# A two-layer conditioned feed-forward kernel: block products for pairs of tiles in place of one tile's dense product

## The reference

```python
x = x + _L0_ffn_ref(_L0_cond_ref(x, ...), ...)
x = x + _L1_ffn_ref(_L1_cond_ref(x, ...), ...)
# _L0_cond_ref: grouped convolution of 9 taps in 4 groups of channels + a row that depends on the sample
# _L0_ffn_ref:  h @ W.T + b, and a low-rank term of which a router picks rank 8, 16, 32 or 64 for each row
# _L1_cond_ref: a 64 x 64 mixing matrix per sample, a softmax mixture of 8, + a bias
# _L1_ffn_ref:  h @ W_base.T + b_base, and 8 experts of rank 16, weighted by a sparsemax router
```

## Time and profile before

| what | value |
|---|---|
| median of three runs (lowest, highest) | 545.91 us (543.35, 546.39) |
| span of the profiled execution | 542.1 us; a time of its own is not given, the median is 3.8 us above its span |
| TensorE matmul busy | 535.2 us, 99% |
| VectorE, ScalarE, GpSimd busy | 243.1, 80.8, 7.6 us |
| bytes by DMA | 56.46 MB, mean 104 GB/s |

### The profile page before, as it was taken

The page is one execution under the profiler, slowest core; times in us unless marked ns, Lnnn a source line. Parts: engine busy times, 40 slices in busy tenths (PEclk is TensorE's granted clock), DMA queues, the critical chain, the costliest instruction groups (busy, mean ns, idle before and its releaser), DMA issues.

```text
span 542.1 us, 9035 instructions
## 1 busy us (share of the span) xinstructions
PE 535.2 (99%) x3401; PEld 532.1 (98%) x3401; DVE 243.1 (45%) x635; ACT 80.8 (15%) x173; POOL 7.6 (1%) x25
## 2 busy tenths in 40 slices
PE   8989999999999999999999999999999999999997
PEld 8989999999999999999999999999999999999997
DVE  1964334344334343343467645454335454434543
ACT  3731101111011111011152100111100111100010
POOL 3010000000000000000000000000000000000000
PEclk9999999999999999999999999999999999999999
DMA  8997633223233222232210222012222102222201
GB/s 271 328 414 236 238 115 118 85 77 109 77 116 116 78 78 96 97 116 81 74 41 39 79 79 77 15 63 77 77 77 77 44 33 77 77 77 77 77 39 40
DMA packets 16057, 56.46 MB, mean 104 GB/s; under 512 B 1915, under 2 KB 3067, under 8 KB 15916
## 3 DMA queue, kind: packets, MB, share of 16 engines
q1 hardware_dynamic: 15980, 56.23, 30.2%
q0 software_dynamic: 64, 0.05, 0.1%
HBM read 39.47 MB, written 16.79 MB: 104 GB/s over the span
## 4 chain that ended last, share of the span: by engine, by line
PE 93%; DMA 4%; ACT 1%; issue 1%; DVE 1%; SPq 0%; POOL 0%; DVEq 0%; POOLq 0%
PE mixp L713 9%; PE acc_a L703 8%; PE acc_a L705 8%; PE acc_a L704 8%; PE acc_b L704 8%; PE acc_b L705 8%; PE acc_b L703 8%; PE acc_c L703 8%; PE acc_c L704 8%; PE acc_c L705 8%; PE mixp L736 5%; DMA w_raw<-in_wcat 2%; DMA ctx_scratch<-ctx_sb 1%; DMA rw<-in_rows 1%; PE utp L756 1%
## 5 line engine op out<-in xcount | busy, mean ns | idle before, releaser
L703 PE MATMUL acc_a<-w_hi,act_hi 128*128 128x388 f32 (+1 forms) x248 | 85.6, 345 | 0.0
L705 PE MATMUL acc_a<-w_hi,act_lo 128*128 128x388 f32 (+1 forms) x248 | 82.8, 334 | 0.0
L704 PE MATMUL acc_a<-w_lo,act_hi 128*128 128x388 f32 (+1 forms) x248 | 82.8, 334 | 0.0
L705 PE MATMUL acc_b<-w_hi,act_lo 128*128 128x388 f32 (+1 forms) x248 | 82.7, 333 | 0.0
L704 PE MATMUL acc_c<-w_lo,act_hi 128*128 128x384 f32 (+1 forms) x248 | 82.7, 333 | 0.0
L704 PE MATMUL acc_b<-w_lo,act_hi 128*128 128x388 f32 (+1 forms) x248 | 82.7, 333 | 0.0
L703 PE MATMUL acc_b<-w_hi,act_hi 128*128 128x388 f32 (+1 forms) x248 | 82.7, 333 | 0.0
L705 PE MATMUL acc_c<-w_hi,act_lo 128*128 128x384 f32 (+1 forms) x248 | 82.6, 333 | 0.0
L703 PE MATMUL acc_c<-w_hi,act_hi 128*128 128x384 f32 (+1 forms) x248 | 82.5, 333 | 0.0
L713 PE MATMUL mixp<-filt,blk 128*128 128x128 f32 x512 | 63.3, 283 | 0.8 <-DMA filt<-in_toep 0.8
L713 PEld LDWEIGHTS mixp<-filt,blk 128*128 128x128 f32 x512 | 62.2, 199 | 0.9 <-DMA blk<-in_xblk 0.9
(11 more groups left out here) (148 smaller groups left out, 521.0 us busy)
## 6 DMA issues: line engine op xcount, KB each, us to landing
blk<-in_xblk SPq DMA_DIRECT2D x16, 516.0 KB, 3.3
xs<-in_x SPq DMA_DIRECT2D x16, 512.0 KB, 3.3
x_scratch<-xs SPq DMA_DIRECT2D x16, 512.0 KB, 2.7
blk<-x_scratch SPq DMA_DIRECT2D x16, 512.0 KB, 4.0
out_dram<-xs SPq DMA_DIRECT2D x15, 512.0 KB, 4.7
w_raw<-in_wcat SPq DMA_DIRECT2D x8, 580.0 KB, 17.0
w_raw<-in_wcat SPq DMA_DIRECT2D x8, 546.0 KB, 7.6
lb_raw<-in_bcat SPq DMA_DIRECT2D x2, 512.0 KB, 13.6
```

Of the source, the lines that this page charges most:

```text
L703: pe.matmul(dst, l_hi, r_hi, start=start, stop=False, skip_group_check=skip)
L704: pe.matmul(dst, l_hi, r_lo, start=False, stop=False, skip_group_check=skip)
L705: return pe.matmul(dst, l_lo, r_hi, start=False, stop=stop, skip_group_check=skip)
```

## The change

Tiles go in pairs: pair g has tiles 2g and 2g+1; pairs 0 to 7 are layer 0, 8 to 15 layer 1. The two tiles' 256 rows, the 1024 inputs in two halves, and 864 (layer 1: 928) output columns in two halves of 432 (464) make a 2 by 2 block product. Pairs 1 to 15 make it with seven products of 12 matmuls each (4 blocks of 128 rows, 3 terms) in place of eight (Strassen's algorithm in Winograd's form). The other 228 (232) columns, with the router's, stay a plain product (`plain`). Pair 0 is still made in the ordinary way (`dense0`).

- Sums of activations, four of 128 x 512 for each pair, are made on GpSimd (`sums`) in place in `mixed`; ScalarE and VectorE split each into hi and lo as they do the activations.
- Sums of layer 0's weights, 16 of 128 x 432, are made on GpSimd behind the split of `lb`; ScalarE and VectorE split them (`split_t`).
- Sums and splits of layer 1's weights are made during pairs 1 to 6, by GpSimd and ScalarE in turn (`prep`), and stored in HBM by ScalarE's queue, 28 blocks of 128 x 464, then 6 of the plain columns and 3 of `lb`. SyncE loads them at the boundary: two halves (hi, lo) of seven slots of 128 x 4 x 464 and of the plain part, 950 KB each, and `lb`.
- Each product's result is added to `xs` by VectorE at once, or left in its bank for the next product; layer 1's mixing matrices (`place_kernels`) go through HBM too.
- In layer 1 GpSimd adds `b_base` to the loaded `x` (`add_base`).
- The loads of `rw` and `bk` are issued by ScalarE, and the context's matmuls are five in place of three.

Constants, and the order of TensorE before and after:

```diff
+HALF = (432, 464)
+PLAIN = (W0COLS - 2 * HALF[0], W1COLS - 2 * HALF[1])
+B11, T3, B21, B22, T1, T2, T4 = range(7)
+PREP_JOBS = ((), ((0, B11), (2, B21)), ((3, B22), (0, T1)), ((1, T3), (3, T2)), ((2, T4),))
+PREP_BASE = 5 * HK
+PREP_STEPS = PREP_BASE + 6
+PREP_FIRST, PREP_LAST = 1, 6
+PREP_A_PAIR = 5
...
-    for k in range(NCH):
-        act_ready(T, k)
-        if k == 0:
-            if mixed_out is None:
-                pe.wait_ge(res_done[PART_C], T - 1)
-        ins = dense(s, cols, PART_C, k)
-    ins.then_inc(hid_done, 1)
...
-    for k in range(NCH):
-        dense(s, cols, PART_A, k)
-        if k == (NCH - 2 if following is not None else NCH - 4):
-            turn_u(T)
-    if following is not None:
-        following(T + 1, 1 - s, pair + s)
-    lora(T, s, PART_C)
-    lora(T, s, PART_A)
-    pe.wait_ge(res_done[PART_B], T)
-    for k in range(NCH):
-        dense(s, cols, PART_B, k)
-    lora(T, s, PART_B)
...
+turn_u(0)
+for k in range(3, 6):
+    dense0(1, k, second)
+pe.wait_ge(lblo_done, 1)
+pe.wait_ge(bias_split, 1)
+h = HALF[0]
+lora(0, b_x, 0, h, c11_done)
+lora(0, b_y, h, 2 * h, c12_done)
+lora(0, b_p[0], 2 * h, D, q_done[0])
+for k in range(6, NCH):
+    dense0(1, k, second)
+conv_half(2, 0, b_m)
+pe.wait_ge(fin11, 1)
+conv_half(2, 1, b_x)
+turn_u(1)
+pe.wait_ge(fin12, 1)
+aggregate(0, b_y)
+lora(1, b_z, 0, h, c21_done)
+lora(1, b_w, h, 2 * h, c22_done)
+lora(1, b_p[1], 2 * h, D, q_done[1])
+pe.wait_ge(sum_done, 5)
+conv_half(3, 0, b_m)
+pe.wait_ge(fin22, 1)
+aggregate(1, b_w)
+pe.wait_ge(fin21, 1)
+conv_half(3, 1, b_z)
...
+for g in range(1, LAST + 1):
+    l = layer(g)
+    h = HALF[l]
+    t1, t2 = 2 * g, 2 * g + 1
+    plain(t1)
+    plain(t2)
+    if g == 1:
+        pe.wait_ge(sum_done, 6)
+    else:
+        pe.wait_ge(fin22, g)
+    product_a(g, P1, b_x, A11, B11)
+    if g < LAST:
+        pe.wait_ge(sum_done, 2 * (t2 + 1))
+        mixture(t1 + 2, 0, b_m)
+    turn_u(t1)
+    pe.wait_ge(sum_done, 2 * (t2 + 1))
+    product_a(g, P2, b_z, A12, B21)
+    if g == 1:
+        pe.wait_ge(agg_read, 2)
+    else:
+        pe.wait_ge(fin12, g)
+    if g < LAST:
+        mixture(t1 + 2, 1, b_y)
+    turn_u(t2)
+    if g == 1:
+        pe.wait_ge(agg_read, 4)
+        pe.wait_ge(tlo_done[T4], HK)
+    else:
+        pe.wait_ge(took_w, g - 1)
+    product_a(g, P4, b_w, A22, T4)
+    if g == 1:
+        pe.wait_ge(tlo_done[T1], HK)
+    if g < LAST:
+        pe.wait_ge(sum_done, 2 * (t1 + 2) + 2)
+    product_s(g, P5, b_y, S1, T1)
+    if g == PAIRS:
+        pe.wait_ge(lb_loaded, 32)
+    lora(t1, b_z, 0, h, c11_done)
+    lora(t1, b_p[0], 2 * h, D, q_done[0])
+    if g < LAST:
+        mixture(t2 + 2, 0, b_m)
+    if g == 1:
+        pe.wait_ge(tlo_done[T2], HK)
+    pe.wait_ge(took_p1, g)
+    product_s(g, P6, b_x, S2, T2, first=False)
+    if g < LAST:
+        pe.wait_ge(fin11, g + 1)
+        mixture(t2 + 2, 1, b_z)
+    lora(t2, b_w, 0, h, c21_done)
+    lora(t2, b_p[1], 2 * h, D, q_done[1])
+    if g == 1:
+        pe.wait_ge(tlo_done[T3], HK)
+    pe.wait_ge(took_u2, g)
+    product_s(g, P7, b_x, S3, T3, first=False)
+    pe.wait_ge(took_p5, g)
+    product_s(g, P3, b_y, S4, B22, first=False)
+    pe.wait_ge(fin21, g + 1)
+    lora(t2, b_x, h, 2 * h, c22_done)
+    lora(t1, b_y, h, 2 * h, c12_done)
```

`conv_half` and `mix_half` are the halves of `conv` and `mix`. The plain product and one block product (x_hi, x_lo are the activations' or the sums' parts, `wb_hi`, `wb_lo` the slots):

```diff
+    for k in range(NCH):
+        if k % HK == 0:
+            pe.wait_ge(alo_done[op], g + 1)
+        x_hi, x_lo = a_hi[:, op, k % HK, :], a_lo[:, op, k % HK, :]
+        pe.matmul(dst, x_hi, wp_hi[:, k, 0:PLAIN[l]], start=(k == 0), stop=False)
+        pe.matmul(dst, x_hi, wp_lo[:, k, 0:PLAIN[l]], start=False, stop=False)
+        ins = pe.matmul(dst, x_lo, wp_hi[:, k, 0:PLAIN[l]], start=False, stop=(k == NCH - 1))
...
+    for k in range(HK):
+        pe.matmul(dst, x_hi[:, k, :], w_hi[:, k, :], start=(first and k == 0), stop=False,
+                  skip_group_check=not first)
+        pe.matmul(dst, x_hi[:, k, :], w_lo[:, k, :], start=False, stop=False, skip_group_check=not first)
+        ins = pe.matmul(dst, x_lo[:, k, :], w_hi[:, k, :], start=False, stop=(k == HK - 1),
+                        skip_group_check=not first)
```

GpSimd:

```diff
+pool.wait_ge(bias_split, 1)
+for kc in range(HK):
+    pool.wait_ge(wlo_done, 2 * (kc + HK) + 1)
+    pool.tensor_tensor(raw_block(kc, 0), raw_block(kc, 1), raw_block(kc, 0), ALU.subtract).then_inc(t_sum, 1)
+    pool.tensor_tensor(raw_block(kc, 1), raw_block(kc, 3), raw_block(kc, 1), ALU.subtract).then_inc(t_sum, 1)
+    pool.wait_ge(t_sum, 4 * kc + 2)
+    pool.tensor_tensor(raw_block(kc, 3), raw_block(kc, 3), raw_block(kc, 0), ALU.subtract).then_inc(t_sum, 1)
+    pool.wait_ge(t_sum, 4 * kc + 3)
+    pool.tensor_tensor(raw_block(kc, 2), raw_block(kc, 2), raw_block(kc, 3), ALU.subtract).then_inc(t_sum, 1)
+for i in (T1, T2, T3, T4):
+    pool.wait_ge(tlo_done[i], HK)
+pool.memset(praw[:, :], 0.0).then_inc(agg_zero, 1)
...
+    pool.wait_ge(alo_done[A21], g + 1)
+    pool.wait_ge(alo_done[A22], g + 1)
+    pool.tensor_tensor(mixed[:, A22, :, :], mixed[:, A21, :, :], mixed[:, A22, :, :], ALU.add).then_inc(s_sum, 1)
...
+    j = prep_jobs_before(step)
+    jobs = prep_jobs_before(step + 1) - j
+    for n in range(jobs):
+        at, width, _ = prep_job(step, n)
+        stage = (j + n) % STAGES
+        pool.wait_ge(prep_hi, j + n + 1)
+        pool.tensor_tensor(stg_lo[:, stage, 0:width], praw[:, at:at + width], hi(stg_hi[:, stage, 0:width]),
+    pool.wait_ge(prep_lo, j + jobs)
+    n = step // 5 * 4
+    if step % 5 == 1:
+        pool.tensor_tensor(prep_block(0), prep_block(1), prep_block(0), ALU.subtract).then_inc(prep_sum, 1)
...
+sums(1)
+for g in range(1, LAST + 1):
+    if g == PAIRS:
+        pool.wait_ge(s_bbase, 16)
+        for q in (0, 1, 3, 2):
+            add_base(q, g)
...
+    if PREP_FIRST <= g <= PREP_LAST:
+        for step in range(PREP_A_PAIR * (g - PREP_FIRST), min(PREP_A_PAIR * (g - PREP_FIRST + 1), PREP_STEPS)):
+            prep(step)
+    if g + 1 != PAIRS:
+        add_base(0, g + 1)
+    if g < LAST:
+        sums(g + 1)
```

VectorE (`take` adds a bank's 432 or 464 columns to `xs`; in layer 1 it waits for `x_biased` of its quarter first, in layer 0 for `x_loaded`):

```diff
+gate0(0)
+split_ut(0)
+split_t(T1, 0)
+dve.wait_ge(c11_done, 1)
+take(b_x, 0, 0, fin11)
+dve.wait_ge(c12_done, 1)
+take(b_y, 1, 0, fin12)
+take_plain(0, 0)
+split_t(T2, 3)
+split_t(T4, 2)
+gate0(1)
+sum_mix(2, 0)
...
+dve.wait_ge(c21_done, 1)
+take(b_z, 2, 0, fin21)
+dve.wait_ge(c22_done, 1)
+take(b_w, 3, 0, fin22)
+take_plain(1, 0)
+split_t(T3, 1)
+sum_mix(3, 0)
+sum_mix(3, 1)
+split_a(A21, 1)
...
+for g in range(1, LAST + 1):
+    split_s(S2, g)
+    split_s(S4, g)
+    gate(2 * g)
+    gate(2 * g + 1)
+    dve.wait_ge(p_done[P1], g)
+    take(b_x, 0, g, took_p1)
+    if g < LAST:
+        sum_mix(2 * g + 2, 0)
+    split_ut(2 * g)
+    if g < LAST:
+        sum_mix(2 * g + 2, 1)
+        split_a(A11, g + 1)
+        split_a(A12, g + 1)
+    split_ut(2 * g + 1)
+    dve.wait_ge(p_done[P5], g)
+    take(b_y, 3, g, took_p5)
+    dve.wait_ge(c11_done, g + 1)
+    dve.wait_ge(took_p1, g)
+    take(b_z, 0, g, fin11)
+    take_plain(0, g)
+    if g < LAST:
+        sum_mix(2 * g + 3, 0)
+    dve.wait_ge(p_done[P6], g)
+    take(b_x, 1, g, took_u2)
+    if g < LAST:
+        sum_mix(2 * g + 3, 1)
+    dve.wait_ge(c21_done, g + 1)
+    take(b_w, 2, g, took_w)
+    take_plain(1, g)
+    if g < LAST:
+        split_a(A21, g + 1)
+        split_a(A22, g + 1)
+    dve.wait_ge(p_done[P7], g)
+    dve.wait_ge(took_w, g)
+    take(b_x, 2, g, fin21)
+    if g < LAST:
+        split_s(S1, g + 1)
+    dve.wait_ge(c22_done, g + 1)
+    dve.wait_ge(took_p5, g)
+    take(b_x, 3, g, fin22)
+    dve.wait_ge(c12_done, g + 1)
+    dve.wait_ge(took_u2, g)
+    take(b_y, 1, g, fin12)
+    if g < LAST:
+        split_s(S3, g + 1)
```

ScalarE, and its stores and copies for the prepared weights:

```diff
+act.wait_ge(consts, N_CONSTS)
+split_ut(0)
+split_t(T1, 0, 1)
+split_t(T2, 3, 3)
+split_t(T4, 2, 4)
+gate_exp(1)
+split_ut(1)
+split_a(A11, 1)
+split_a(A12, 1)
+act.wait_ge(dense0_done, 2)
+split_t(T3, 1, 2)
+act.wait_ge(agg_zero, 1)
+place_kernels(0)
+place_kernels(1)
+split_a(A21, 1)
+split_a(A22, 1)
...
+    split_s(S2, g)
+    split_s(S4, g)
+    gate_exp(2 * g)
+    gate_exp(2 * g + 1)
+    split_ut(2 * g)
+    if prepares:
+        prep(step)
+    if g < LAST:
+        split_a(A11, g + 1)
+        split_a(A12, g + 1)
+    split_ut(2 * g + 1)
+    if prepares:
+        prep(step + 1)
+        prep(step + 2)
+        prep(step + 3)
+        prep(step + 4)
+    if g < LAST:
+        split_a(A21, g + 1)
+        split_a(A22, g + 1)
+        split_s(S1, g + 1)
+        split_s(S3, g + 1)
...
+        act.wait_ge(prep_lo, j + n + 1)
+        act.dma_start(dst[0], hi(stg_hi[:, stage, 0:width])).then_inc(prep_stored[stage], 16)
+        act.dma_start(dst[1], hi(stg_lo[:, stage, 0:width])).then_inc(prep_stored[stage], 16)
...
+        act.wait_ge(prep_raw, prep_loads(step))
+        if prep_sums_needed(step):
+            act.wait_ge(prep_sum, prep_sums_needed(step))
+        if j + n >= STAGES:
+            act.wait_ge(prep_stored[stage], 32 * ((j + n) // STAGES))
```

(53 more changed lines are left out.)

1138 lines of the change are left out of this document (608 added, 530 removed).

## The result

The changed kernel takes **600.88 us** (median of four, 598.72 to 601.85) against 545.52 for the kernel before in the same job: ratio **1.102**, 95% interval 1.099 to 1.106. The forecast had the sign; 600.88 lies outside its range of 530 to 588, and the loss of 55 us is nearly three times the 19 us forecast. The profiled execution took 598.72, its span 597.0.

The account below looks back on a forecast made before the run. TensorE's stream was taken as the time. Span 542.1 - 39.5 (columns) + 12.2 + 7.2 + 15.0 + 19 (waits) + 0.8 (end) + 4 (clock) gave 561; the median, 3.8 above span, 565 us; range 530 to 588.

Parts of the forecast that it names:

- The sign: Whole kernel: the change makes it slower, 565 us against 545.52; slower was given 70%.
- rival (b): GpSimd's subtraction costs what VectorE's does, 0.6 us for 464 columns, shortening the chain of sums: 533 us; 15%.
- Rival (a): The columns alone decide and every new wait is hidden: 503 us of span, 507 us; 6%.
- Rival (c): The boundary doesn't stall, as transfers pass each other and `x` comes before it is wanted: 545 us; 9%.
- I take 1 us each: TensorE's half clock after four new waits (5.5, 6.7, 4.3, 19 us): +4 us, each bounded by 0 and 6.1.
- Rival (d): Half clock for long after each new wait, from waits of about 3 us: 24 us in place of 4, 585; 10%.
- The columns: TensorE's matmuls in pairs 1 to 15: 2.55 us saved in each of 7 pairs, 2.7 in each of 8, -39.5 us.
- the bound of -34: Smallest saving allowed for TensorE's columns, whose range was -34 to -46 us.
- rival (e): Plain matmuls save nothing for being short, 113 ns each: 5 us more, 570 us; inside the forecast, which had 60%.
- The boundary: Pair 8: TensorE waits at tile 17's turning for `x`, queued behind layer 1's weight loads: 19 us.
- The end: Kernel's end: the last two additions instead of one, +0.8 us.
- the 39 us: Boundary: 16.3 MB of weight pieces and `lb` at the full queue's 418 GB/s take 39 us.

Follow-up runs that it names:

- e2: Changed kernel with fifteen unneeded matmuls of ones put before TensorE's wait for `fin21` in pairs 1 to 5: 586.74 us, ratio 1.077.
- e3: Changed kernel with pair 8's activations loaded ahead of T2, T3, B22 and `lb` on SyncE's queue: 584.70 us, ratio 1.074.
- e10: Changed kernel, boundary alone: T4, T1 loaded early, activations' stores without waits between, pair 8's VectorE split before taking the first product: 579.81 us, ratio 1.067.
- e16: e15 with the boundary's block loads cut to 32 of 464 columns, so layer 1 uses layer 0's weights in the rest: 528.77 us, ratio 0.970.
- e15: e14 with pair 2's rows loaded ahead of the 1 MB store of aggregation kernels, and the base row's load back in pair 7: 547.98 us, ratio 1.007.
- e13: e14 with T1's two pieces loaded behind pair 8's rows and aggregation matrices: 555.66 us, ratio 1.022.
- e5: Changed kernel with the preparation's steps spread over pairs 1 to 7, three in pairs 1 and 2, five in 3 to 5: 583.49 us, ratio 1.074.
- e6: Changed kernel with boundary loads in order of use: T4 late in pair 7, four other slots and `lb` behind the activations: 589.46 us, ratio 1.083.
- e7: Changed kernel with pair 0's splits in order of use and each pair's first gate ahead of the S2 and S4 splits: 595.88 us, ratio 1.094.
- e14: A 549.61 us version combining the order edits, with pair 1's second gate also ahead of S1 and S3 and the base row loaded in pair 6: 554.10 us.

## Why the prediction was wrong, and where it was right

**Right.** The sign, and the places of the waits, each behind work in one stream in order. Pair 1's first turning was forecast for 69.4 + 12 + 4.3 = 85.7 us and came at 85.4, which is partly luck: its four waits were 1.8, 6.1, 1.2 and 3.6 us, 12.7 in all, where 19.4 were forecast, and what made up for it was work at the lower clock, dearer matmuls and a wait at tile 0's turning. In a preparing pair ScalarE's run was forecast at 14.1 us and took 14.8; the wait at `fin21` at 3.6, measured 3.4:

```profile
207.36 1.06 ACT L656 CAST stg_hi<-praw 128x464 fp32r<-128x464 f32 x2
...
217.30 1.06 ACT L656 CAST stg_hi<-praw 128x464 fp32r<-128x464 f32 x2 [4.54 <-POOL praw L530]
...
222.14 1.14 ACT L588 CAST a_hi<-mixed 128x512 fp32r<-128x512 f32 x2
```

GpSimd's subtractions cost 1.15 us in a row and 1.18 in the mean, so rival (b) falls; its 512-column sums took 1.29, two of the four 1.46 and 1.62. Additions from PSUM took 0.60 (432 columns) and 0.64 us (464) beside GpSimd's work and without it. The Trainium skill (SBUF — State Buffer, "Who interferes with whom") exempts a VectorE instruction with at most one input in SBUF, and the trace agrees. Rival (a) falls by 58 us of waits. Rival (c) is refuted by the wait of 24.4 us and by the queue, SyncE's issue times of the last blocks, of two stores and of the activations:

```profile
345.84 0.79 SPq L442 DMA_DIRECT2D wb_lo<-wb_scratch  x1
...
347.73 0.92 SPq L318 DMA_DIRECT2D x_scratch<-xs  x2
361.31 1.74 SPq L313 DMA_DIRECT2D xs<-x_scratch  x4
```

The activations were issued 13.6 us after the stores, and VectorE took the first product at 365.3, having stood 32.4 us for them.

**Wrong, by 36 us of span, in three terms of the sum.**

The clock, 21.9 us. The step "I take 1 us each" counted four waits and priced them near the lower end. The clock fell after the wait of 3.4 us in each of the five preparing pairs too, for which the step had nothing, though the forecast itself had four waits of 3.6 us there: e2 took 14.1 us off. The forecast held waits for nearly free because TensorE lags other engines; the rows show 213 ns in place of 111 for some 5.5 us behind a wait of 3.4. Rival (d), at 10%, had the mechanism. That its 24 us is what was measured is luck: it had four falls of 6.1 us each, the trace has nine, which cost 2.7 us each in the mean outside of waits. By its own condition, waits of about 3 us, it left out the four in the preparing pairs. The Trainium skill (TensorE: Matmul & The Clock Gate, "What's actually happening") has throttled as the default state, which activity releases; the rows agree. With the clock so priced the sum was rival (d)'s 585, still 16 us short.

The columns, 10.3 us. "105 and 107 ns" for the plain matmuls were 112, and "195" and "208.5" for the block products were 199.5 and 215 in the mean: 195.5 and 211 within a product, and up to 90 ns more for its first matmul (300 against 210 above). A pair saves 2.0 and 1.9 us, not 2.55 and 2.7, and the bound of -34 was too narrow: rival (e) priced the short matmuls, and no term the first one of a product. Neither the shorter run nor the new bank makes it dear: behind another product it costs 195 and 210 ns in the mean, as the others do, behind a mixing or a turning 283 to 302. The kernel before has it too, 254 and 262 ns once a tile behind the turning; now a pair has three or four. Counted in before as well, a pair saves 2.05 and 2.1 us. Why a matmul is dear in that place, no run shows.

The waits, 4.5 us. The boundary was 24.4 + 3.0 us (turning and mixing) and not 19. Pair 5 kept its wait, 3.3 us where I had 0.6: its step 23 loads `bcat`, issued at 253.0, and the copy of step 24 stands for the landing until 258.1. Those of pairs 0 and 1 were 6.7 us less than summed. The end, 0.3 for 0.8, and the step from span to median (an execution takes 1.7 us more than its own span, 598.72 and 597.0; the 3.8 set a median against one execution's span) are small.

The boundary's mechanism was right for the changed kernel ("behind all that in SyncE's order"): e3 and e10 took off 16 and 21 us by order. But the 39 us that the step worked out for 16.3 MB against a pair of 28 us meant more than a wait that can be ordered away: e16 shows 19 us of bytes under it, and the full DMA engines of e15 and the waits that only moved in e13 agree.

## What to carry to other kernels

Where TensorE is busy all the time, a saving in its columns is worth only what the new waits leave of it, and each new wait of about 3 us has to be priced twice, for itself and for the half-rate matmuls that may follow (2.8 us a pair here). Work for idle engines costs nothing where its steps stand in ones and twos in idle places, and a wait where they stand in a run before an operand: five steps a pair took 37.6 us in the one way and 31.2 in the other. Before counting on order at a stage boundary, divide its bytes by the queue's rate; where that is longer than the stage, order takes off only a part (21 us here) and then moves the wait (19 us stayed).

## What the runs showed that was not expected

- Filling a wait with useless matmuls won 14 us, 2.8 us a pair, with no other change.
- Clearing waits was worth less than the waits in pairs 0 and 1 (4.1 us for 7 to 9 us cleared), as the next operand was due there; the gains of e5, e6 and e7, in three different places, added up.
- The first matmul of a product cost up to 90 ns more behind a mixing or a turning, and nothing more behind another product.
- One load of a row repeated over the partitions (0.5 MB of SBUF) took 8.5 us from issue to landing in pair 6, in which the DMA engines were 90% busy at 301 GB/s; pair 7's loads came later, and e14's wait for `agg` was 10.3 us in place of 6.3.
